# Attention and gated feed-forward on one Trainium2 core: one transpose per key tile for both halves, the second key tile filled by a DMA, the queries' halves swapped between the score tiles

## The chip, the cores and the metric

The kernel runs on one core of one Trainium2 chip. The metric is the device time of one execution in microseconds (us). Before the change the median of 3 runs is 1196.5 us (1196.28 to 1198.25).

## The reference

```python
def _L0_xattn_ref(hidden_q, kv_c, Wq, w_kc_q, w_kc_kv, W_qr, W_kr, Wo):
    q_big = jnp.einsum('bshk,hkq->bshq', (hidden_q @ Wq.T).reshape(b, s, H, K), w_kc_q)
    kv_rope = kv_c * cos[None] + _rotate_half(kv_c) * sin[None]
    q_r = jnp.einsum('bshq,hqr->bhsr', q_big, W_qr)
    k_r = jnp.einsum('bld,hdr->bhlr', kv_rope, W_kr)
    attn = jax.nn.softmax(jnp.einsum('bhsr,bhlr->bhsl', q_r, k_r), axis=-1)
    ctx_c = jnp.einsum('bhsl,bld->bhsd', attn, kv_rope)
    ctx_lat = jnp.einsum('bhsd,hkd->bshk', ctx_c, w_kc_kv)
    return ctx_lat.reshape(b, s, H * K) @ Wo.T
...
x = x + _L0_xattn_ref(_layernorm(x), ctx_512, ...)
x = x + _L0_ffn_ref(_layernorm(x), ...)
```

There are 8 batches of 256 queries of width 256. Each attends over 1601 keys of width 64, which all 16 heads share. The feed-forward part takes the last row of each batch through four gelu steps, spreads the result over the rows, gates it and normalises.

## The kernel before

At the start all weights are folded, so that a head's query is 64 wide and scores are a product with the rotated keys themselves. Scores are wanted more exactly than one 16-bit product gives, so keys and queries are split into a high f16 half and a low one (what the high half leaves), and a score is high·high + high·low + low·high.

The main loop runs over 8 batches (n), in each over 8 pairs of heads (p), in each over 13 tiles of 128 keys (t). A pair's queries fill 512 columns. For each tile TensorE issues, in this order, the scores (`L739` with `k_hi`, `L740` with `k_lo`, into `ps_s`), a product whose maximum over keys a later pair needs (`L610`, `L613`, into `ps_m`, read by VectorE at `L934`), perhaps one extra piece of work, and 12 products of probabilities with keys for the tile six steps back (`p_kv`, `L658`, `L661`, `L668`). ScalarE makes the probabilities (`L459`); their low halves are made by GpSimd on 11 tiles of 13 and by VectorE on the others (`make_low`, `L207`). PSUM bank `ps_x` is shared by the extra pieces; TensorE waits in `take_x` until its last user has read it.

GpSimd prepares the keys of the next batch between its other work (`keys`, `L311`, slots written out by hand in `KEY_SLOTS`): it rotates them and stores for each tile `k3` = [high 64, ones, low 64, the factor 16, 31 zeros], 162 columns. TensorE turns them in four pieces (`keys_turned`), placed by hand: piece 0 (high, tiles 0 to 7) at p 3, t 12; piece 1 (high, tiles 8 to 12) at p 5, t 6; pieces 2 and 3 (low) at p 6, t 6 and t 12. In pieces 0 and 1 each tile takes two transposes, `L544` to all 128 PSUM rows and `L545`, which writes the high half once more over rows 64 to 127. Pieces 2 and 3 take one transpose for each tile (`L547`). ScalarE copies each piece to SBUF (`copy_keys`). So `k_hi` holds [high; high] on 128 rows and `k_lo` holds [low; 16; zeros] on 96. The queries come to `qq` by DMAs that SyncE issues (`move_queries`): `qq[:, 0]` is [high; low] and `qq[:, 1]` is [high; negated maximum, by `copy_row`; zeros]. For batch 0 all this is done in the head of the kernel, in banks of their own.

The lines of `keys_turned` (TensorE), which the change touches most:

```python
if i < 2:
    pe.transpose(psum[:, c:c + 128], k3[par][:, t, 0:128], identh[:, :])
    mm = pe.transpose(psum[DC:128, c:c + 128], k3[par][:, t, 0:DC], identh[:, :])
else:
    mm = pe.transpose(psum[0:96, c:c + 128], k3[par][:, t, LOW:LOW + 96], identh[:, :])
```

Of the kernel before, what the change touches and what calls it, by code (L numbers as in the profile page):

```python
# [39 lines left out]
KC = 162  # L40
ONE, LOW, FACTOR = DC, DC + 1, 2 * DC + 1
# [13 lines left out]
def build_xattn_ffn(nc, x, kv, kv_last, cos_n, sin_n, ident_in, sel_in, wq, wkcq_t, wkckv, wqr, wkr_t, wo_t,  # L55
                    in_gamma, in_beta, agg_w, agg_b, pn_gamma, pn_beta, d1_w, d1_b, d2_w, d2_b,
                    bc_w, bc_b, gate_w, gate_b, out_gamma, out_beta, out):
    with ExitStack() as ctx:
# [19 lines left out]
        k_hi = [sb(f"k_hi{i}", [128, LP], F16) for i in range(2)]  # L78
        k_lo = [sb(f"k_lo{i}", [96, LP], F16) for i in range(2)]
# [80 lines left out]
        prep, kt_done, kt_copied = sem("prep"), sem("kt_done"), sem("kt_copied")  # L160
# [27 lines left out]
        def first_key_bank(i):  # L188

            return (ps_o[:, 0, :].bitcast(F16), ps_m[:, 0, :].bitcast(F16), ps_m[:, 1, :].bitcast(F16), ps_xh)[i]  # L190
# [34 lines left out]
        def _(sp):  # L225
# [18 lines left out]
            def move_queries(p, g):  # L244
# [5 lines left out]
                for h in range(2):  # L250
                    for j in range(2):
                        sp.dma_start(d[0:64, j, h * S:(h + 1) * S], q_hi[r][64 * h:64 * h + 64, :]).then_inc(in_qq[r], 16)
                sp.wait_ge(ql_done, g + 1)
                for h in range(2):
                    sp.dma_start(d[64:128, 0, h * S:(h + 1) * S], q_lo[r][64 * h:64 * h + 64, :]).then_inc(in_qq[r], 16)

            move_queries(0, 0)
            move_queries(1, 1)
            sp.dma_start(gw[:, :, :], gate_w.rearrange("(t p) m -> p t m", p=128)).then_inc(in_gate, 16)
# [10 lines left out]
            def batch(n, par):  # L270
# [7 lines left out]
                for p in range(NP - 2 if last(n) else NP):  # L278
                    move_queries((p + 2) % NP, n * NP + p + 2)

# [11 lines left out]
        def _(pool):  # L292
            def keys(n, par, k):
# [6 lines left out]
                else:  # L300
# [69 lines left out]
        def _(act):  # L370
# [70 lines left out]
            for i in range(4):  # L441
                copy_keys(0, 0, i, first_key_bank(i))
# [6 lines left out]
            def batch(n, par):  # L449
                for p in range(NP):  # L450
                    g = n * NP + p
                    started = not (first(n) and p == 0)
                    for t in range(KT):
# [6 lines left out]
                        if t == 6 and not last(n) and p in (5, 6):  # L460
                            copy_keys(n + 1, 1 - par, p - 4)
# [7 lines left out]
                        if t == 12 and not last(n) and p in (3, 6):  # L469
                            copy_keys(n + 1, 1 - par, 0 if p == 3 else 3)  # L470
# [65 lines left out]
        def _(pe):  # L536
            def keys_turned(n, par, i, psum=ps_xh):

                pe.wait_ge(prep, n * PREP_OPS + (6 if i % 2 == 0 else 12))
                for t in range(8) if i % 2 == 0 else range(8, KT):  # L540
                    c = (t % 8) * 128
                    if i < 2:

                        pe.transpose(psum[:, c:c + 128], k3[par][:, t, 0:128], identh[:, :])  # L544
                        mm = pe.transpose(psum[DC:128, c:c + 128], k3[par][:, t, 0:DC], identh[:, :])  # L545
                    else:
                        mm = pe.transpose(psum[0:96, c:c + 128], k3[par][:, t, LOW:LOW + 96], identh[:, :])  # L547
                mm.then_inc(kt_done, 1)

# [35 lines left out]
            for i in range(3):  # L585
                keys_turned(0, 0, i, first_key_bank(i))
# [15 lines left out]
            def maxima(par, p, g, j):  # L602
# [4 lines left out]
                if j < MX_OPS - 1:  # L607
                    a = (j // 3) * 128
                    c = (j % 3) * 512
                    mm = pe.matmul(ps_m[:, j % 3, :], qq[p % 4][:, 0, a:a + 128], k_hi[par][:, c:c + 512], start=True, stop=True)  # L610
                else:
                    for i in range(4):
                        mm = pe.matmul(ps_m[:, 1, i * LAST:(i + 1) * LAST], qq[p % 4][:, 0, i * 128:(i + 1) * 128],  # L613
                                       k_hi[par][:, L - LAST:L], start=True, stop=True)
# [15 lines left out]
            keys_turned(0, 0, 3)  # L630
            pe.wait_ge(kt_copied, 3)
# [11 lines left out]
            pe.wait_ge(kt_copied, 4)  # L643
# [6 lines left out]
            def p_kv(n, par, p, t):  # L650
# [9 lines left out]
                for q in range(4):  # L660
                    pe.matmul(d[:, q // 2, q % 2, 0:DC], probs_hi(t)[:, q * 128:(q + 1) * 128], k3[par][:, t, LOW:LOW + DC],  # L661
# [53 lines left out]
            def batch(n, par):  # L715
# [9 lines left out]
                for p in range(NP):  # L725
# [3 lines left out]
                    for t in range(KT):  # L729
# [3 lines left out]
                        if t == 0:  # L733
                            pe.wait_ge(mrow_copied, g + 1)
                            if p == 0 and not first(n):
                                pe.wait_ge(kt_copied, n * 4 + 4)
# [7 lines left out]
                        if t >= KT - EARLY and not (last(n) and p >= NP - 2):  # L744
                            if t == KT - EARLY:
                                pe.wait_ge(in_qq[p % 2], n * (QQ_DMAS * 4) + QQ_DMAS * ((p + 2) // 2 + 1))
                                if p == NP - 2:
                                    pe.wait_ge(kt_copied, n * 4 + 6)
# [4 lines left out]
                        if t == 6 and not last(n) and p in (5, 6):  # L753
                            take_x((kt_copied, n * 4 + (4 + p - 3)))
                            keys_turned(n + 1, 1 - par, p - 4)
# [9 lines left out]
                        if t == 12:  # L765
# [88 lines left out]
        def _(dve):  # L854
# [371 lines left out]
```

## Time and profile before

| what | value |
| --- | --- |
| runs | 1196.28, 1196.5, 1198.25 us, median 1196.5 |
| the profiled execution | 1192.87 us |
| its span, first to last instruction | 1191.1 us |
| mean granted TensorE clock | 0.961 of full |
| TensorE busy | 1104.9 us, 93% |
| GpSimd, VectorE, ScalarE busy | 889.8, 882.1 and 670.9 us |

The engines are named PE (TensorE matmul), PEld (its weight load), DVE (VectorE), ACT (ScalarE), POOL (GpSimd), SP (SyncE). L547 is line 547 of the kernel. The ends of matmuls are modelled, so that back-to-back ones overlap in the records: the cost of one is the distance between starts, not its duration. Idle time of an engine that sets nothing costs nothing.

### The profile page before, as it was taken

Reading aid. Unit: us, or ns where it says so; the run is one execution under the profiler, and the core shown is the slowest. Engines: PE = TensorE matmul, PEld = TensorE weight load, DVE = VectorE, ACT = ScalarE, POOL = GpSimd, SP = SyncE. Lnnn points to the kernel's source line nnn. Section 1 sums busy time; section 2 is a strip of 40 time slices with the busy share of each in tenths; the row PEclk is TensorE's granted clock in tenths of the full one; section 3 lists DMA queues with packets and bytes.
Section 4 is the critical chain, followed back from the end, with each engine's and each line's share of the span. In section 5 each row is a group of like instructions: output and inputs, shape, how many; then the busy total and the mean of one; then the engine's idle time right before and its main releaser. Section 6 shows DMA issues by size and latency. Waiting matters only on the chain.

```text
span 1191.1 us, 39790 instructions
## 1 busy us (share of the span) xinstructions
PE 1104.9 (93%) x14852; PEld 735.9 (62%) x14852; DVE 882.1 (74%) x1573; ACT 670.9 (56%) x1195; POOL 889.8 (75%) x956
## 2 busy tenths in 40 slices
PE   5879999999999998999999999999999999999361
PEld 4636666666666665666666666666676666667240
DVE  4377778777787777777878687777877787887448
ACT  1445566566665665565656665566656565567322
POOL 0329887898788976798788877897879877787713
PEclk9989999999999999999999999999999999999655
DMA  9020001000100001000100001000100020000002
GB/s 331 40 78 14 14 14 27 14 16 15 30 16 14 12 14 33 14 14 12 30 16 16 15 16 29 12 15 16 29 13 13 14 86 16 15 15 3 1 2 71
DMA packets 41288, 34.69 MB, mean 29 GB/s; under 512 B 7608, under 2 KB 38648, under 8 KB 40640
## 3 DMA queue, kind: packets, MB, share of 16 engines
q1 hardware_dynamic: 40512, 27.79, 8.3%
q10 hardware_dynamic: 576, 4.19, 1.0%
q8 instruction: 130, 2.13, 0.7%
q14 instruction: 70, 0.57, 0.2%
HBM read 17.27 MB, written 2.10 MB: 16 GB/s over the span
## 4 chain that ended last, share of the span: by engine, by line
PE 85%; DVE 7%; issue 3%; DMA 2%; ACT 1%; POOL 1%; SPq 1%; DVEq 0%; ACTq 0%; POOLq 0%
PE ps_s L740 14%; PE ps_s L739 14%; PE ps_m L610 13%; PE ps_o L658 8%; PE ps_o L661 8%; PE ps_o L668 8%; PE ps_x L598 3%; PE ps_x L684 3%; PE ps_x L621 2%; DVE mx L934 1%; PE ps_x L545 1%; PE ps_x L676 1%; PE ps_x L544 1%; DMA plo_all<-wqr_dram 1%; PE ps_x L711 1%
## 5 line engine op out<-in xcount | busy, mean ns | idle before, releaser
L207 POOL TENSOR_TENSOR plo_all<-big 128x512 f16<-128x512 f32 x640 | 683.3, 1085 | 213.8 <-ACT big L459 213.0
L934 DVE TENSOR_REDUCE mx<-ps_m 128x1 f32<-128x512 f32 (+1 forms) x832 | 544.7, 666 | 218.6 <-PE ps_m L610 188.2
L459 ACT ACTIVATE big<-ps_s 128x512 f32<-128x512 f32 x768 | 458.4, 598 | 342.2 <-PE ps_s L740 341.1
L739 PE MATMUL ps_s<-qq,k_hi 128*128 128x512 f16 (+1 forms) x832 | 316.2, 380 | 5.6 <-issue 5.6
L740 PE MATMUL ps_s<-qq,k_lo 96*128 96x512 f16 (+1 forms) x832 | 318.0, 382 | 0.0
L610 PE MATMUL ps_m<-k_hi,qq 128*128 128x512 f16 x768 | 293.1, 382 | 5.1 <-ACT k_lo L378 2.3
L658 PEld LDWEIGHTS ps_o<-k,big 128*128 128x128 bf16 x3072 | 184.9, 98 | 119.8 <-issue 1.1
L661 PE MATMUL ps_o<-k,big 128*128 128x64 f16 x3072 | 219.8, 193 | 0.0
L668 PE MATMUL ps_o<-k,plo_all 128*128 128x65 f16 x3072 | 218.2, 193 | 0.0
L658 PE MATMUL ps_o<-k,big 128*128 128x65 f16 x3072 | 218.1, 193 | 0.0
L207 DVE TENSOR_TENSOR plo_all<-big 128x512 f16<-128x512 f32 x128 | 172.3, 1346 | 0.0
L661 PEld LDWEIGHTS ps_o<-k,big 128*128 128x128 bf16 x3072 | 146.5, 98 | 0.0
L668 PEld LDWEIGHTS ps_o<-k,plo_all 128*128 128x128 f16 x3072 | 144.8, 97 | 0.1
L610 PEld LDWEIGHTS ps_m<-k_hi,qq 128*128 128x128 f16 x768 | 76.0, 99 | 103.6 <-DVE mx L934 9.9
L739 PEld LDWEIGHTS ps_s<-qq,k_hi 128*128 128x128 f16 (+1 forms) x832 | 81.7, 98 | 7.4 <-issue 6.9
L740 PEld LDWEIGHTS ps_s<-qq,k_lo 96*128 96x128 f16 (+1 forms) x832 | 82.4, 99 | 0.9 <-issue 0.6
L311 POOL TENSOR_TENSOR tables<-tables 128x256 f32<-128x256 f32 (+3 forms) x64 | 60.6, 947 | 27.7 <-DMA tables<-kv_last_dram 27.1
L207 POOL TENSOR_TENSOR plo_last<-pr_last 65x512 f16<-65x512 f32 x64 | 66.3, 1036 | 0.9 <-ACT pr_last L459 0.9
L598 PE MATMUL ps_x<-xnt,mw 128*128 (+1 forms) x384 | 52.2, 272 | 2.4 <-DVE mw L913 1.4
L598 PEld LDWEIGHTS ps_x<-xnt,mw 128*128 128x128 f16 x384 | 37.1, 97 | 20.9 <-DVE mw L913 1.6
L459 ACT ACTIVATE pr_last<-ps_s 65x512 f32<-65x512 f32 x64 | 38.0, 594 | 13.9 <-PE ps_s L740 13.6
L378 ACT ACTIVATE qq<-ps_x 1x512 f16<-1x512 f32 x64 | 37.7, 589 | 5.8 <-PE ps_x L621 4.2
(200 smaller groups left out, 998.4 us busy)
## 6 DMA issues: line engine op xcount, KB each, us to landing
qq<-q_hi SPq DMA_DIRECT2D x256, 32.0 KB, 1.9
qq<-q_lo SPq DMA_DIRECT2D x128, 32.0 KB, 1.9
tables<-kv_dram SPq DMA_DIRECT2D x8, 384.0 KB
big<-wq_dram ACTq DMA_DIRECT2D x1, 2048.0 KB, 15.5
xs<-x_dram SPq DMA_DIRECT2D x4, 512.0 KB, 18.0
big<-wo_t_dram SPq DMA_DIRECT2D x1, 2048.0 KB, 13.1
tables<-d_w_dram SPq DMA_DIRECT2D x2, 1024.0 KB, 6.9
out_dram<-big SPq DMA_DIRECT2D x8, 256.0 KB, 2.2
```

What stands on the lines that cost most here:

```text
L207: eng.tensor_tensor(probs_lo(t)[0:r, :], probs(t)[0:r, :], probs_hi(t)[0:r, :], ALU.subtract).then_inc(done, 1)
L311: pool.tensor_tensor(*ops[k % 6]).then_inc(prep, 1)
L378: return act.activation(out_, in_, ACT.Copy, **kw)
L459: act.activation(probs(t)[0:r, :], ps_s[0:r, (p * KT + t) % 2, :], ACT.Exp, scale=1.0 / SC).then_inc(p_done, 1)
L598: mm = pe.matmul(ps_x[:, 0:S], mw[wi][:, mt, p * 128:(p + 1) * 128], xn_hl[xi][:, bass.ds(n * S + mt * B * S, S)], start=(i == 0), stop=(i ...
L610: mm = pe.matmul(ps_m[:, j % 3, :], qq[p % 4][:, 0, a:a + 128], k_hi[par][:, c:c + 512], start=True, stop=True)
L658: pe.matmul(d[:, q // 2, q % 2, :], probs_hi(t)[:, q * 128:(q + 1) * 128], k3[par][:, t, 0:OW], start=(t == 0 and q == 0), stop=False, ski ...
L661: pe.matmul(d[:, q // 2, q % 2, 0:DC], probs_hi(t)[:, q * 128:(q + 1) * 128], k3[par][:, t, LOW:LOW + DC], start=False, stop=False, skip_g ...
L668: mm = pe.matmul(d[:, q // 2, q % 2, :], probs_lo(t)[:, q * 128:(q + 1) * 128], k3[par][:, t, 0:OW], start=False, stop=(t == KT - 1), skip ...
L739: pe.matmul(ps_s[0:r, j % 2, :], k_hi[par][:, c], qq[p % 4][:, 0, :], start=True, stop=False)
L740: pe.matmul(ps_s[0:r, j % 2, :], k_lo[par][:, c], qq[p % 4][0:96, 1, :], start=False, stop=True).then_inc(st_done, 1)
L934: dve.tensor_reduce(o, i, AX.X, ALU.max).then_inc(mx_read, 1)
```

## The change

The tile `k3` becomes [ones, high 64, low 64], 130 columns, so that high and low lie side by side. One transpose for each key tile gives [high; low] on 128 rows; pieces 2 and 3 and the second transposes are gone, and with them half of ScalarE's key copies. `k_hl` takes the place of `k_hi`. `k_hx`, in the place of `k_lo`, is [high; 16; zeros]: its high rows are filled by a DMA from `k_hl`, issued by SyncE after each copy (`move_keys`), its other 32 rows are written once at the start. The queries are swapped to fit: `qq[:, 0]` is [high; high], `qq[:, 1]` is [low; negated maximum; zeros]. The first scores of a batch wait for the DMAs (`in_kx`) instead of the copies. The maxima are now taken over high·high + low·high instead of high·high + high·low.

```diff
-KC = 162
-ONE, LOW, FACTOR = DC, DC + 1, 2 * DC + 1
+KC = 130
+ONE, HIGH, LOW = 0, 1, DC + 1
...
-        k_hi = [sb(f"k_hi{i}", [128, LP], F16) for i in range(2)]
-        k_lo = [sb(f"k_lo{i}", [96, LP], F16) for i in range(2)]
+        k_hl = [sb(f"k_hl{i}", [128, LP], F16) for i in range(2)]
+        k_hx = [sb(f"k_hx{i}", [96, LP], F16) for i in range(2)]
...
                     for j in range(2):
-                        sp.dma_start(d[0:64, j, h * S:(h + 1) * S], q_hi[r][64 * h:64 * h + 64, :]).then_inc(in_qq[r], 16)
+                        sp.dma_start(d[64 * j:64 * j + 64, 0, h * S:(h + 1) * S], q_hi[r][64 * h:64 * h + 64, :]).then_inc(in_qq[r], 16)
                 sp.wait_ge(ql_done, g + 1)
                 for h in range(2):
-                    sp.dma_start(d[64:128, 0, h * S:(h + 1) * S], q_lo[r][64 * h:64 * h + 64, :]).then_inc(in_qq[r], 16)
+                    sp.dma_start(d[0:64, 1, h * S:(h + 1) * S], q_lo[r][64 * h:64 * h + 64, :]).then_inc(in_qq[r], 16)
+
+            def move_keys(n, par, i):
+                sp.wait_ge(kt_copied, n * 2 + (i + 1))
+                sp.dma_start(k_hx[par][0:64, key_half(i)], k_hl[par][0:64, key_half(i)]).then_inc(in_kx, 16)
...
             move_queries(1, 1)
+            for i in range(2):
+                move_keys(0, 0, i)
...
+                    if not last(n) and p in (3, 5):
+                        move_keys(n + 1, 1 - par, (p - 3) // 2)
...
-                    (k3[par][:, c, 0:DC], raw[:, c, :], rot[:, c, :], ALU.add),
+                    (k3[par][:, c, HIGH:HIGH + DC], raw[:, c, :], rot[:, c, :], ALU.add),
                     (raw[:, c, :], raw[:, c, :], rot[:, c, :], ALU.add),
-                    (k3[par][:, c, LOW:LOW + DC], raw[:, c, :], k3[par][:, c, 0:DC], ALU.subtract),
+                    (k3[par][:, c, LOW:LOW + DC], raw[:, c, :], k3[par][:, c, HIGH:HIGH + DC], ALU.subtract),
...
-                act.wait_ge(kt_done, n * 4 + (i + 1))
-                c = slice(0, 1024) if i % 2 == 0 else slice(1024, LP)
-                d = k_hi[par] if i < 2 else k_lo[par]
-                r = 128 if i < 2 else 96
-                copy(d[0:r, c], psum[0:r, 0:c.stop - c.start]).then_inc(kt_copied, 1)
+                act.wait_ge(kt_done, n * 2 + (i + 1))
+                c = key_half(i)
+                copy(k_hl[par][:, c], psum[:, 0:c.stop - c.start]).then_inc(kt_copied, 1)
...
-                        if t == 6 and not last(n) and p in (5, 6):
-                            copy_keys(n + 1, 1 - par, p - 4)
+                        if t == 6 and not last(n) and p == 5:
+                            copy_keys(n + 1, 1 - par, 1)
...
-                        if t == 12 and not last(n) and p in (3, 6):
-                            copy_keys(n + 1, 1 - par, 0 if p == 3 else 3)
+                        if t == 12 and not last(n) and p == 3:
+                            copy_keys(n + 1, 1 - par, 0)
...
-                pe.wait_ge(prep, n * PREP_OPS + (6 if i % 2 == 0 else 12))
-                for t in range(8) if i % 2 == 0 else range(8, KT):
+                pe.wait_ge(prep, n * PREP_OPS + 6 * (i + 1))
+                for t in range(KT)[HALVES[i]]:
                     c = (t % 8) * 128
-                    if i < 2:
-
-                        pe.transpose(psum[:, c:c + 128], k3[par][:, t, 0:128], identh[:, :])
-                        mm = pe.transpose(psum[DC:128, c:c + 128], k3[par][:, t, 0:DC], identh[:, :])
-                    else:
-                        mm = pe.transpose(psum[0:96, c:c + 128], k3[par][:, t, LOW:LOW + 96], identh[:, :])
+                    mm = pe.transpose(psum[:, c:c + 128], k3[par][:, t, HIGH:HIGH + 128], identh[:, :])
...
-            for i in range(3):
+            for i in range(2):
...
-            keys_turned(0, 0, 3)
-            pe.wait_ge(kt_copied, 3)
+            pe.wait_ge(kt_copied, 2)
             pe.wait_ge(in_qq[0], QQ_DMAS)
...
+                            if p == 0:
+                                pe.wait_ge(in_kx, n * 32 + 32)
...
-                        pe.matmul(ps_s[0:r, j % 2, :], k_hi[par][:, c], qq[p % 4][:, 0, :], start=True, stop=False)
-                        pe.matmul(ps_s[0:r, j % 2, :], k_lo[par][:, c], qq[p % 4][0:96, 1, :], start=False, stop=True).then_inc(st_done, 1)
+                        pe.matmul(ps_s[0:r, j % 2, :], k_hl[par][:, c], qq[p % 4][:, 0, :], start=True, stop=False)
+                        pe.matmul(ps_s[0:r, j % 2, :], k_hx[par][:, c], qq[p % 4][0:96, 1, :], start=False, stop=True).then_inc(st_done, 1)
...
-                            elif p in (3, 6) and not last(n):
-                                i = 0 if p == 3 else 3
-                                take_x((kt_copied, n * 4 + (4 + i + 1)))
-                                keys_turned(n + 1, 1 - par, i)
+                            elif p == 3 and not last(n):
+                                take_x((kt_copied, n * 2 + 3))
+                                keys_turned(n + 1, 1 - par, 0)
...
-                pad(k3[i][:, :, FACTOR:FACTOR + 1], SC)
-                pad(k3[i][:, :, FACTOR + 1:KC], 0.0)
+                pad(k_hx[i][64:96, :], 0.0)
+            for i in range(2):
+                pad(k_hx[i][64:65, :], SC, 7)
```

## Rows read from the trace of the kernel before

**Rows 1.** The page's busy times: engine, us (share of the span), instructions.

```profile
PE 1104.9 (93%) x14852; PEld 735.9 (62%) x14852; DVE 882.1 (74%) x1573; ACT 670.9 (56%) x1195; POOL 889.8 (75%) x956
```

**Rows 2.** A window: busy us of PE, PEld, DVE, ACT, POOL, granted clock, DMA share, GB/s.

```profile
208.00:336.00 128.00, 127.68 (x1778) 85.50 (x1777) 98.99 (x171) 77.77 (x139) 106.33 (x114) 1.00 0.07 18
```

**Rows 3.** Waits of TensorE from 100 to 1095 us: total, times, longest.

```profile
PE ps_s L739 <- issue: 5.6, 2, 3.0
PE ps_x L676 <- DVE ctx_m L957: 1.6, 7, 0.2
```

**Rows 4.** Timeline of TensorE around pieces 0 and 1 (keys for batch 1): start, us, what.

```profile
137.18 0.22 PE L544 MATMUL ps_x<-identh,k 128*128 128x128 f16 x1
137.33 0.24 PE L545 MATMUL ps_x<-identh,k 128*64 128x128 f16 x1
...
139.86 0.29 PE L658 MATMUL ps_o<-k,big 128*128 128x65 f16 x4
...
162.30 0.23 PE L544 MATMUL ps_x<-identh,k 128*128 128x128 f16 x1
...
163.98 0.20 PE L658 MATMUL ps_o<-k,big 128*128 128x65 f16 x1
```

**Rows 5.** The chain that ended last, at pieces 2 and 3: start, us on it.

```profile
178.56 0.45 PE ps_x L547 x8
...
185.65 0.28 PE ps_x L547 x5
```

**Rows 6.** Weight loads of L547 and of L544: ns min/median/max.

```profile
L547 PEld LDWEIGHTS ps_x<-identh,k x96: 120/124/125, 62.0 to 964.0; 128*96 128x96 f16 x96
...
L544 PEld LDWEIGHTS ps_x<-identh,k x91: 95/96/97, 137.0 to 940.2; 128*128 128x128 f16 x91
```

**Rows 7.** Timeline of the head, TensorE and GpSimd.

```profile
36.69 0.92 POOL L311 TENSOR_TENSOR k<-tables 128x320 f16<-128x320 f32 x1
...
38.64 0.78 POOL L311 TENSOR_TENSOR k<-tables,k 128x320 f16<-128x320 f32 x1
...
46.76 0.22 PE L544 MATMUL ps_o<-identh,k 128*128 128x128 f16 x1 [0.74 <-issue]
...
51.81 3.42 PE L590 MATMUL ps_s<-plo_all,nw 128*128 128x128 f32 x16
...
58.43 0.83 PE L598 MATMUL ps_x<-xnt,mw 128*128 128x256 f16 x6 [1.42 <-DVE mw L913]
```

**Rows 8.** A window of the head, columns as in rows 2.

```profile
51.80:55.00 3.20, 3.20 (x18) 3.20 (x17) 0.50 (x1) 0.60 (x1) 0.00 (x0) 0.54 0.00 0
```

**Rows 9.** VectorE in the head: its wait for the input, its memsets (ns min/median/max).

```profile
DVE st_f L878 <- DMA xs<-x_dram: 13.7, 1, 13.7
...
L858 DVE MEMSET qq<- x4: 272/272/272, 2.7 to 3.6; 32x256 uint32 x4
```

**Rows 10.** Timeline of batch 1, pairs 3 to 5: GpSimd's lead over TensorE.

```profile
271.02 1.04 POOL L207 TENSOR_TENSOR plo_all<-big 128x512 f16<-128x512 f32 x1 [0.77 <-ACT big L459]
...
273.33 2.04 POOL L207 TENSOR_TENSOR plo_all<-big 128x512 f16<-128x512 f32 x2
...
278.49 0.28 PE L668 MATMUL ps_o<-k,plo_all 128*128 128x65 f16 x4
```

**Rows 11.** Timeline of batch 1: copies, query DMAs, the tile that needs them.

```profile
266.40 1.02 ACT L378 ACTIVATE k_hi<-ps_x 128x1024 f16<-128x1024 f16 x1 [2.20 <-PE ps_x L545]
...
271.22 0.39 ACT L378 ACTIVATE q_hi<-ps_x 128x256 f16<-128x256 f32 x1 [0.28 <-PE ps_x L598]
...
286.55 2.39 SPq L252 DMA_DIRECT2D qq<-q_hi  x4
288.99 1.23 SPq L255 DMA_DIRECT2D qq<-q_lo  x2
...
294.55 0.38 PE L610 MATMUL ps_m<-k_hi,qq 128*128 128x512 f16 x1
```

**Rows 12.** Landing of the query DMAs, all of the span.

```profile
DMA to landing us min/median/max: 1.7/1.9/3.5
```

More of the change, by code:

```diff
@@ L159, in build_xattn_ffn @@
             sem(s) for s in ("ln", "ln_dev", "xn_act", "xn_dve", "xt_done", "xt_copied", "xt_low"))
-        prep, kt_done, kt_copied = sem("prep"), sem("kt_done"), sem("kt_copied")
+        prep, kt_done, kt_copied, in_kx = (sem(s) for s in ("prep", "kt_done", "kt_copied", "in_kx"))
         q_done, qh_done, ql_done = sem("q_done"), sem("qh_done"), sem("ql_done")
@@ L188, in first_key_bank, with key_half @@
         def first_key_bank(i):
-            return (ps_o[:, 0, :].bitcast(F16), ps_m[:, 0, :].bitcast(F16), ps_m[:, 1, :].bitcast(F16), ps_xh)[i]
+            return (ps_o[:, 0, :].bitcast(F16), ps_m[:, 0, :].bitcast(F16))[i]
+        def key_half(i):
+            return slice(0, 1024) if i == 0 else slice(1024, LP)
         def sums(r):
@@ L440, in _ @@
             high_part(1, 1)
-            for i in range(4):
+            for i in range(2):
                 copy_keys(0, 0, i, first_key_bank(i))
@@ L609, in maxima @@
                     c = (j % 3) * 512
-                    mm = pe.matmul(ps_m[:, j % 3, :], qq[p % 4][:, 0, a:a + 128], k_hi[par][:, c:c + 512], start=True, stop=True)
+                    mm = pe.matmul(ps_m[:, j % 3, :], qq[p % 4][:, 0, a:a + 128], k_hl[par][:, c:c + 512], start=True, stop=True)
                 else:
@@ L613, in maxima @@
                         mm = pe.matmul(ps_m[:, 1, i * LAST:(i + 1) * LAST], qq[p % 4][:, 0, i * 128:(i + 1) * 128],
-                                       k_hi[par][:, L - LAST:L], start=True, stop=True)
+                                       k_hl[par][:, L - LAST:L], start=True, stop=True)
                 mm.then_inc(mx_done, 1)
@@ L642, in _ @@
                         mm.then_inc(fold, 1)
-            pe.wait_ge(kt_copied, 4)
             max_row(0)
@@ L660, in p_kv @@
                 for q in range(4):
-                    pe.matmul(d[:, q // 2, q % 2, 0:DC], probs_hi(t)[:, q * 128:(q + 1) * 128], k3[par][:, t, LOW:LOW + DC],
+                    pe.matmul(d[:, q // 2, q % 2, HIGH:OW], probs_hi(t)[:, q * 128:(q + 1) * 128], k3[par][:, t, LOW:LOW + DC],
                               start=False, stop=False, skip_group_check=True)
@@ L747, in batch @@
                                 if p == NP - 2:
-                                    pe.wait_ge(kt_copied, n * 4 + 6)
+                                    pe.wait_ge(kt_copied, n * 2 + 4)
                             maxima(par if p < NP - 2 else 1 - par, p + 2, g + 2, t - (KT - EARLY))
@@ L752, in batch @@
                             project(1 - par, (1,))
-                        if t == 6 and not last(n) and p in (5, 6):
-                            take_x((kt_copied, n * 4 + (4 + p - 3)))
-                            keys_turned(n + 1, 1 - par, p - 4)
+                        if t == 6 and not last(n) and p == 5:
+                            take_x((kt_copied, n * 2 + 4))
+                            keys_turned(n + 1, 1 - par, 1)
                         if t == 3 and not (last(n) and p >= NP - 2):
@@ L864, in _ @@
                 pad(k3[i][:, :, ONE:ONE + 1], 1.0)
-                pad(k3[i][:, :, FACTOR:FACTOR + 1], SC)
-                pad(k3[i][:, :, FACTOR + 1:KC], 0.0)
+                pad(k_hx[i][64:96, :], 0.0)
+            for i in range(2):
+                pad(k_hx[i][64:65, :], SC, 7)
             for i in range(4):
@@ L956, in normalise @@
                 dve.wait_ge(inv_done, g + 1)
-                dve.tensor_tensor(ctx_m[:, :, :, :].rearrange("p s h d -> p h s d"), d[:, :, :, 0:DC],
+                dve.tensor_tensor(ctx_m[:, :, :, :].rearrange("p s h d -> p h s d"), d[:, :, :, HIGH:OW],
                                   inv[:, :, :].unsqueeze(3).to_broadcast([128, 2, ST, DC]), ALU.mult).then_inc(ctx_norm, 1)
```

2 lines of the change are left out of this document (removed).

## The prediction

> **What bounds the kernel now.** I read the page's busy times first [rows 1]: TensorE is busy for 93% of the span, the next engine for 75%. A share over the span can hide a stage with another limit, so I cut out a stretch of one batch's length [rows 2]: TensorE is busy for 127.68 of 128 us at full clock, GpSimd for 106.33, VectorE for 98.99, ScalarE for 77.77. The waits of TensorE between 100 and 1095 us, nearly the whole main loop, settle it [rows 3]: 5.6 us where it waits for nothing that the trace shows (two gaps), and 1.6 us for VectorE in seven waits of 0.2 us. So in the loop TensorE's own work sets the time: what is taken off it comes off the end, as long as the others keep up. The reader is to see that nobody else's removed work counts there.
>
> The last thing to read is how much the removed work takes. Matmul records overlap, so I take distances between starts. Piece 0 (8 tiles, 16 transposes) begins at 137.18 and the next kind of work at 139.86: 2.68 us. Piece 1 (5 tiles, 10 transposes) goes from 162.30 to 163.98: 1.68 us [rows 4]. Both are 0.335 us for each pair of transposes, or 0.168 us each. Pieces 2 and 3, with one transpose for each tile, stand in the chain that ended last with 0.45 us for 8 and 0.28 us for 5 [rows 5], 0.056 us each. The alternation between L544 over all rows and L545 over the upper 64 makes a transpose three times as dear as in an unbroken run of like ones.
>
> **The change, part by part.**
>
> *Transposes in the loop.* Pieces 0 and 1 stay, with one transpose for each tile, in an unbroken run into the same rows: the form of pieces 2 and 3, so 0.45 and 0.28 us. The old pieces 2 and 3 go. A batch saves (2.68 - 0.45) + (1.68 - 0.28) + 0.45 + 0.28 = 4.36 us. Keys are turned in the loop for 7 batches: 7 x 4.36 = 30.5 us.
>
> What isn't seen in the trace is the new transpose itself: 128 columns wide as its weights go and starting one element into the row. The nearest row is L547: 96 wide, starting at element 65, also odd. Its weight load takes 124 ns and that of L544, 128 wide at an even start, 96 ns [rows 6]; at a spacing of 56 ns the former is evidently hidden behind the stream before. I take 56 ns. From one side, the most that a cheaper one could give is all of it, 13 x 0.056 x 8 = 5.8 us. From the other, the old mean of 168 ns would cost 13 x 0.112 x 8 = 11.6 us. The middle case, loads of 124 ns one after another, is a rival below.
>
> On that spacing the Trainium skill speaks against me: its page "TensorE: Matmul & The Clock Gate", section "Back-to-back issue gap", gives about 81 ns for a matmul of 128 columns in a stream of weight load and matmul pairs, against about 56 ns for an isolated gap. This trace has 56 ns for just such pairs of transposes. By the page's 81 ns the 104 new transposes would cost an estimated 104 x 0.025 = 2.6 us more.
>
> *Transposes in the head.* The four pieces of batch 0 lie between 46.76, the first, and 51.81, where the fold that follows begins [rows 7] (of piece 3, five transposes, issued later, I say nothing: it lies before a wait for DMAs). That is 5.05 us for 34 transposes; the 13 new ones take 0.73. The keys themselves were ready at 39.4, so GpSimd isn't what is waited for, and the chain goes on from the fold by way of ScalarE and VectorE to the queries at 58.43, which all move forward with it. I take 4.3 us. The clock was granted at 0.54 in the window of the fold [rows 8], so the same work could take some 1.5 us less or, where a fall comes at another place, more. I keep 4.3 and put 1.5 us on both sides.
>
> *ScalarE.* Two of four key copies go, 14 in the loop of about 1.0 or 0.7 us. ScalarE is busy for 78 of 128 us [rows 2] and TensorE doesn't wait for it [rows 3]: nothing. In the head the two first copies end earlier, but the queries' DMAs stand in the same wait: nothing.
>
> *GpSimd's key operations.* Same count and sizes. The high half is now written at an odd element. The low half always was, and its operation takes 0.78 us where the even one takes 0.92 [rows 7], so I see no price. If there were one, GpSimd would pay it out of the slack reckoned below.
>
> *Memsets.* Two of 32 x 1664 and two of 1 x 1664 f16 come, against four small ones. 32 x 256 words take 0.27 us [rows 9], so 832 words take about 0.85 us each, 3.4 us in all; VectorE then waits 13.7 us for the input [rows 9], and GpSimd starts the keys only after their own load. Nothing. Without that cover it would be 3 us, once.
>
> *The DMAs.* Two more for each batch, 128 and 80 KB, are issued on SyncE's queue behind the queries of pairs 3 and 5. SyncE waits there for the copy of the keys. Behind it stand the queries of the next pair. In batch 1 the copy ends at 267.42, and the next queries are ready to move at 271.61 [rows 11]: SyncE is free again 4.2 us before, less 0.6 us for issuing one DMA (four take 2.39). The wait of TensorE for them comes at the first tile of the next batch, two pairs or more later, against 1.9 us, at most 3.5, for a landing of 32 KB [rows 12]. Even four times the longest is well inside. In the head they are issued after the queries of pair 1 and are needed after the 13 maxima of pair 0: hidden too.
>
> *What comes nearer to binding.* GpSimd, at pairs 3 to 5, where four key operations and the root's steps stand. Piece 0 gets shorter by 2.23 us, so TensorE comes that much sooner. GpSimd has 0.77 us of idle time before 271.02 which it can use up [rows 10], so its lead falls by about 1.5 us. The low half of tile 4 is ready at 274.35 (the first of the two from 273.33) and used at 278.49: a lead of 4.1 us, which falls to about 2.7. It holds, and over the batch GpSimd has 106 us of work in the 123.6 that remain. VectorE has 99. The query DMAs: the last of pair 5 is issued at 290.22, lands at about 292.1, and is used at 294.55 [rows 11, 12]; piece 1 takes 1.4 us out of that, leaving about 1.0, which is what pairs without a piece have today. TensorE's wait for in_qq costs nothing in those [rows 3].
>
> **The sum.** 30.5 + 4.3 = 34.8 us. The profiled execution took 1192.87 us, 1.8 around its span; it would be 1158.1. The median of the runs is 3.6 us above it: 1196.5 - 34.8 = 1161.7 us.
>
> **The rivals.** *The weight loads don't hide.* The new transposes are 128 wide at an odd start; if each waits for a load like L547's 124 ns, 104 x 0.068 = 7.1 us are lost: 1168.8 us. For it: the load is the longer of the two. Against it: the same load hides today. By the 81 ns that the Trainium skill's page "TensorE: Matmul & The Clock Gate" gives in that section, a weaker form of this, it would be an estimated 1164.3 us.
>
> *The cover gives way.* GpSimd's low halves come late after piece 0. From the point where its lead is under 2.2 us instead of 4.1, TensorE waits once a batch for what is missing, at most the 2.23 us saved there: 15.6 us in all, 1177.3 us; half of it is 1169.5. For it: 83% busy against the 75% that the page shows. Against it: the lead above.
>
> *All given back.* Another engine's round for a pair is the true beat and TensorE's work only fills it. It would be 1196 us. Rows 3 speak against it: TensorE would have idled somewhere.
>
> *Slower, by SyncE's queue.* A move of keys holds up the queries behind it. It is free if it ends in the 4.2 us; each us over that, and over the 1.0 us that the queries have in hand, is a us of waiting at the maxima. With 14 moves it eats the gain only if each is late by 2.5 us beyond both, about 7.7 us after the copy, and ends slower beyond: at 9 us after the copy, 14 x (9 - 5.2) = 53 us, 1215 us. A landing of 3.5 us at most [rows 12] speaks against it.
>
> **How the numbers follow.** Forecast 0.76, unhidden loads 0.08, cover gives way in part 0.10, all given back 0.03, slower 0.03. The range goes from 1157.5 (1.5 us for the head's clock, and a part of the 5.8) to 1169.5, where the unhidden loads and half of the lost cover lie. A difference of 0.2%, 2.4 us, is about what can be told from none. Faster 0.94, same 0.03, slower 0.03.
>
> **What would show it.** TensorE with 104 transposes of keys, all of one form and 56 ns apart; pieces of 0.45 and 0.28 us, and a batch of about 123.3 us; still no wait of TensorE in the loop above 2 us in sum; the fold in the head beginning at about 47.5. Wrong if the transposes stand 80 ns or more apart, if L668 waits for GpSimd or L610 for a query DMA once a batch, or if the first scores of a batch wait for k_hx.

## The result, and the profile after

The kernel after takes 1167.5 us in the median of 4 runs (1164.5 to 1168.2), against 1196.4 us of the kernel before. The ratio is 0.9751, with a 95% interval from 0.9731 to 0.9771. 28.9 us are saved where 34.8 were forecast. The profiled execution took 1167.40 us, 25.5 less than that of before.

The page of the kernel after, its busy times, answers to [rows 1]:

```profile
PE 1073.1 (92%) x14644; PEld 714.8 (61%) x14644; DVE 886.5 (76%) x1573; ACT 657.9 (56%) x1179; POOL 890.4 (76%) x956
```

TensorE has 208 instructions less and 32 us less of work. GpSimd has what it had; VectorE has 4 us more, about what the four memsets of `k_hx` at the start take (0.75 to 1.45 us each). The timeline of TensorE in the kernel after, at piece 0 and at piece 1, answers to [rows 4, 5]:

```profile
128.67 0.61 PE L552 MATMUL ps_x<-identh,k 128*128 128x128 f16 x8
129.11 0.28 PE L660 MATMUL ps_o<-k,big 128*128 128x65 f16 x4
...
273.73 0.38 PE L614 MATMUL ps_m<-k_hl,qq 128*128 128x512 f16 x1
274.29 0.45 PE L552 MATMUL ps_x<-identh,k 128*128 128x128 f16 x5 [0.19 <-DVE q_lo L925]
274.58 0.28 PE L660 MATMUL ps_o<-k,big 128*128 128x65 f16 x4
```

Eight transposes take 0.44 us and five 0.29, 55 to 58 ns each, at an odd start and 128 columns wide. Ahead of piece 1 stands something new: its first transpose could have begun at 273.95, one spacing of 0.22 us after L614, and begins at 274.29, 0.34 us late. It waits for VectorE's low queries. Now the waits of TensorE in the loop, from 90 to 1070 us, as in [rows 3]:

```profile
PE ps_s L741 <- issue: 12.6, 2, 6.7
PE ps_x L678 <- DVE ctx_m L959: 1.6, 7, 0.2
PE ps_m L614 <- DMA qq<-q_lo: 1.6, 4, 0.6
PE ps_x L552 <- DVE q_lo L925: 0.9, 5, 0.2
```

The first line had 5.6 us in [rows 3]. It is two gaps again, and they have more than doubled. The third line is new: small waits for query DMAs, the two of 0.6 us in the pairs that follow the gaps. The chain that ended last, in the kernel after, goes straight through one of them:

```profile
436.10 0.60 ACT pr_last L469
436.70 5.87 issue
442.57 0.61 PE ps_s L741
443.18 0.43 PE ps_s L742
```

And windows of the gap and of what follows (columns as in rows 2):

```profile
436.50:442.50 6.00, 0.14 (x5) 0.02 (x1) 0.60 (x2) 0.19 (x1) 1.31 (x2) 0.80 0.06 15
442.50:447.00 4.50, 4.43 (x32) 2.49 (x33) 1.38 (x2) 1.20 (x2) 1.71 (x2) 0.51 0.01 4
447.00:452.00 5.00, 5.00 (x69) 3.30 (x67) 4.16 (x6) 2.77 (x5) 2.68 (x4) 1.00 0.05 13
```

TensorE stands still, with nothing that the profile shows holding it, and the others nearly so (GpSimd, the busiest, works for 1.31 of 6 us). Behind the gap TensorE runs at half clock (0.51 granted, the 1.2 GHz level) for about 4.5 us. The place is where TensorE's instruction stream returns to the top of its loop: the 8 batches are batch 0, a loop of three rounds of two batches, and batch 7, so the loop returns before batches 3 and 5. The traffic of the kernel after in that gap (436.4 to 442.6) is instruction fetch, on two queues:

```profile
q14 instruction: 7, 0.06, 3.5%
q8 instruction: 2, 0.03, 2.5%
```

Which of them is TensorE's can be told from the pages of the straight kernels below. With TensorE alone in a straight line q8 has 116 packets in the whole execution for the 129 of the kernel after, and q14 has 70 as before. With all engines in a straight line q14 has 42, and q8 stays at 116. So q8 fetches TensorE's instructions, and q14 those of other engines: in the kernel after with TensorE straight, the same window again holds 7 packets of q14, and TensorE works on.

To see where the whole difference went, I took the starts of the query products, one for each pair at its tile 3, and compared the distances (us, pair by pair, in the profiled executions):

```
interval that holds                    before          after
piece 0 (pair 3), 7 batches            17.09 to 17.34  14.85 to 14.86
piece 1 (pair 5), batches 1 to 5       17.81           16.75 to 16.77
the same, batch 0; batch 6             16.35; 17.81    14.95; 16.43
old pieces 2 and 3 at pair 6           15.13 to 15.14  14.40 to 14.41
first pair of batch 0                  14.70          13.10
loop return before batch 3             19.21           22.56, next pair 15.17 for 14.40
loop return before batch 5             17.13           23.70, next pair 15.16 for 14.40
pairs with none of these               equal within 0.4, most within 0.02
```

| term | forecast | in the profiled executions |
| --- | --- | --- |
| pieces in the loop | 30.5 | 15.9 + 8.1 + 5.1 = 29.1 |
| head, first key transpose (46.76; 45.27) to first scores (79.39; 72.30) | 4.3 | 5.6 |
| pair 0 of batch 0 (14.70; 13.10) | 0 | 1.6 |
| start of the first key transpose (arrival of inputs) | 0 | 1.5 |
| the two loop returns with the pair behind each | 0 | -11.5 |
| the rest | 0 | -0.8 |
| sum | 34.8 | 25.5 |

The start of the first key transpose is chance: it lies between 45.27 and 46.89 us in the profiles of the kernel after and its variants.

Against the medians the step at the loop is smaller, since other runs of the kernel before took about 1196 us and its profiled one only 1192.87.

### The profile page after: what moved, and what is told of

The parts are those of the page before. It is cut to its first block, busy times and chain, and to the rows that moved or that the text cites. A ratio compares the mean times of both kernels' runs of the same rounds, so it can differ in the third digit from the quotient of the medians.

```text
span 1165.6 us, 39347 instructions
## 1 busy us (share of the span) xinstructions
PE 1073.1 (92%) x14644; PEld 714.8 (61%) x14644; DVE 886.5 (76%) x1573; ACT 657.9 (56%) x1179; POOL 890.4 (76%) x956
## 4 chain that ended last, share of the span: by engine, by line
PE 81%; DVE 8%; issue 4%; DMA 4%; SPq 2%; ACT 1%; POOL 1%; DVEq 0%; ACTq 0%; POOLq 0%
PE ps_s L742 14%; PE ps_s L741 14%; PE ps_m L614 13%; PE ps_o L660 8%; PE ps_o L663 8%; PE ps_o L670 8%; PE ps_x L602 3%; PE ps_x L686 3%; DMA qq<-q_lo 2%; DVE mx L936 2%; PE ps_x L625 2%; SPq L255 1%; PE ps_x L678 1%; PE ps_x L713 1%; DMA plo_all<-wqr_dram 1%
## 5 line engine op out<-in xcount | busy, mean ns | idle before, releaser
L741 PE MATMUL ps_s<-qq,k_hl 128*128 128x512 f16 (+1 forms) x832 | 317.3, 381 | 12.6 <-issue 12.6
L742 PE MATMUL ps_s<-qq,k_hx 96*128 96x512 f16 (+1 forms) x832 | 319.0, 383 | 0.0
L614 PE MATMUL ps_m<-k_hl,qq 128*128 128x512 f16 x768 | 293.8, 383 | 6.7 <-DMA qq<-q_lo 5.5
L614 PEld LDWEIGHTS ps_m<-k_hl,qq 128*128 128x128 f16 x768 | 76.4, 100 | 107.6 <-DVE mx L936 13.9
L741 PEld LDWEIGHTS ps_s<-qq,k_hl 128*128 128x128 f16 (+1 forms) x832 | 81.7, 98 | 14.4 <-issue 13.8
L742 PEld LDWEIGHTS ps_s<-qq,k_hx 96*128 96x128 f16 (+1 forms) x832 | 82.6, 99 | 1.0 <-issue 0.8
L323 POOL TENSOR_TENSOR tables<-tables 128x256 f32<-128x256 f32 (+3 forms) x64 | 55.1, 861 | 27.1 <-DMA tables<-kv_last_dram 26.5
```

What stands on the lines that cost most here:

```text
L323: pool.tensor_tensor(*ops[k % 6]).then_inc(prep, 1)
L741: pe.matmul(ps_s[0:r, j % 2, :], k_hl[par][:, c], qq[p % 4][:, 0, :], start=True, stop=False)
L742: pe.matmul(ps_s[0:r, j % 2, :], k_hx[par][:, c], qq[p % 4][0:96, 1, :], start=False, stop=True).then_inc(st_done, 1)
```

## The experiments

The theories. **A**: the transposes are worth what was forecast, and what is missing went into TensorE's return to the top of its loop. **B**: it is the new wait for `k_hx` at that place, or a loss spread over the loop. In the diffs "..." stands for lines or text left out.

**TensorE in a straight line**, in the kernel after:

```diff
-            batches(pe, batch)
+            for n in range(B):
+                batch(n, n % 2)
```

> The kernel after, with TensorE's 8 batches written out in a straight line; the other four engines keep their loop. Theory A: the missing microseconds are TensorE's return to the top of its loop, before batches 3 and 5, where it stood still for 5.9 and 6.7 us and then ran at half the clock (the two pairs took 8.2 and 9.3 us more than the others, and each next pair 0.8 us more). Then both gaps go, no pair 0 takes over 14.6 us, and the time falls by 17 to 19 us to about 1150. Theory B: the gap is the wait for k_hx at the first tile of a batch, or the loss is spread over the loop: the gaps stay, and the time is within 3 us of 1167.5.

Measured: 1151.5 us (1150.0 to 1152.6), ratio to the kernel before 0.9632 (0.9608 to 0.9656). The gaps are gone; the intervals of 22.56 and 23.70 us are 15.42 and 15.41. A holds. It had said 14.6 at most, though, and 17 to 19 us for the 16.0 measured: 1.0 us stays at each place, most of it a wait of TensorE for ScalarE (0.85 and 0.83 us), which here still has its loop. TensorE's waits from 90 to 1055 us have no "issue" any more; the longest is

```profile
PE ps_s L741 <- ACT big L469: 1.7, 2, 0.8
```

**The same in the kernel before**:

> The kernel before, with TensorE's 8 batches in a straight line. Theory A: its two gaps (3.0 and 2.6 us in the profiled run, pairs 4.8 and 2.7 us too long) go as well, and the time falls by 7 to 12 us to 1185 to 1189. The difference to the straight form of the kernel after is then the transposes alone: 30.5 in the loop less 1.8 for a wait on the low queries, and 4 to 7 in the head, 33 to 36 us. Theory B: no fall in either, and a difference of 29 us as between the looped kernels.

Measured: 1188.7 us (1185.6 to 1189.6), ratio 0.9945 (0.9922 to 0.9968). So the loop costs the kernel before 7.3 us and the kernel after 16.0, and without it the change is worth 1188.7 - 1151.5 = 37.2 us by the medians, a little above the 33 to 36 expected, and 33.9 us by the two profiled executions. In these it is 958.1 against 928.7 us from the query product of pair 1 in batch 0 to the last one, 29.5 for the 30.5 of the forecast.

**The order of the transposes**, in the kernel before: all first ones of a piece, then all second ones.

```diff
+                    for t in ts:
...
                         pe.transpose(psum[:, c:c + 128], k3[par][:, t, 0:128], identh[:, :])
+                    for t in ts:
...
                         mm = pe.transpose(psum[DC:128, c:c + 128], k3[par][:, t, 0:DC], identh[:, :])
```

> The kernel before, with the same transposes of pieces 0 and 1 in another order: first all onto 128 rows, then all second ones onto rows 64 to 127. Theory A: the alternation is what makes them dear, and in two runs each takes 0.056 us: piece 0 takes 0.9 us and piece 1 0.56 instead of 2.68 and 1.68, which is 2.9 us a batch, 20.4 in the loop and 2.9 in the head: 1173 us. Theory B: the transposes onto the upper rows are dear in themselves, about 0.28 us each: the pieces stay at 2.7 and 1.7 us and the time at 1196.

Measured: 1213.4 us (1212.6 to 1215.8), ratio 1.0157 (1.0130 to 1.0183): slower, against both theories. The transposes did get cheap: the timeline of TensorE has this for the second half of piece 0,

```profile
257.16 0.63 PE L547 MATMUL ps_x<-identh,k 128*64 128x128 f16 x8
257.73 0.29 PE L662 MATMUL ps_o<-k,big 128*128 128x65 f16 x4
```

8 in 0.57 us, 71 ns each, and the interval with piece 0 fell from 17.09 to 15.53 us. It is the alternation that was dear. But pair 4, which follows, took 21.0 to 21.9 us instead of 14.84 in batches 1 to 6, because of a wait for VectorE. That is 40.1 us in all, and 1213.4 less 40.1 is 1173.3, where theory A had expected the kernel. The timelines of VectorE and of GpSimd in that run:

```profile
262.61 7.84 DVE L207 TENSOR_TENSOR plo_all<-big 128x512 f16<-128x512 f32 x1
```

```profile
261.23 3.03 POOL L207 TENSOR_TENSOR plo_all<-big 128x512 f16<-128x512 f32 x3
264.23 0.86 POOL L311 TENSOR_TENSOR tables<-tables 128x320 f32<-128x320 f32 x1
265.06 2.03 POOL L207 TENSOR_TENSOR plo_all<-big 128x512 f16<-128x512 f32 x2
267.05 0.85 POOL L311 TENSOR_TENSOR k<-tables 128x320 f16<-128x320 f32 x1
267.87 2.03 POOL L207 TENSOR_TENSOR plo_all<-big 128x512 f16<-128x512 f32 x2
273.94 1.04 POOL L207 TENSOR_TENSOR plo_all<-big 128x512 f16<-128x512 f32 x1 [4.04 <-ACT big L459]
```

A low half of VectorE that takes 0.68 to 2.2 us elsewhere in this run, mostly 1.4, lasts 7.84 us, from within an unbroken stretch of GpSimd's work to its end at 269.90 and a little beyond. Both engines read two operands in SBUF. I called this **theory C**: the operation gets no turn while GpSimd has no pause, and it depends on where in the stretch it begins. The missing pause alone isn't enough: in the kernel after GpSimd works unbroken from 253.03 to 279.12, and the low halves that VectorE begins at 256.21, 264.10 and 271.05 last 0.93, 1.14 and 2.18 us. The first of these is the one that answers to the stalled one, 0.71 us behind the start of GpSimd's three low halves where the stalled one began 1.38 us behind it. But the second begins 1.45 us behind the start of such a group and isn't stalled, so the distance alone doesn't decide it either. The Trainium skill, page "SBUF — State Buffer", section "SBUF: two separate sides", has a lock on the ports that the two engines share, held for a whole instruction by whoever starts first. The trace agrees that one blocks the other, but VectorE stood here through more than six instructions of GpSimd.

**The second transposes put back**, in the kernel after:

```diff
-                    mm = pe.transpose(psum[:, c:c + 128], k3[par][:, t, HIGH:HIGH + 128], identh[:, :])
+                    pe.transpose(psum[:, c:c + 128], k3[par][:, t, HIGH:HIGH + 128], identh[:, :])
+                    mm = pe.transpose(psum[DC:128, c:c + 128], k3[par][:, t, HIGH:HIGH + DC], identh[:, :])
```

> The kernel after, with a second transpose of each key tile put back behind the first, onto rows 64 to 127, as before (these rows then hold the high half, so the products with the low half of the keys are lost). Theory A: 13 pairs a batch at 0.335 us instead of 13 transposes at 0.056 us: 3.6 us a batch, 25.4 in the loop and 3.6 in the head, 1196 us; everything but the transposes (copies, DMAs, swapped queries) is worth nothing. Theory B: they cost what a like one costs, 5.8 us in all, 1173 us.

Measured: 1187.1 us (1186.6 to 1191.9). Theory A had said 1196, theory B 1173. The intervals of pieces 0 and 1 are those of the kernel before, 17.10 and 17.82 us, so the pairs of transposes cost 2.25 and 1.07 us a batch over the kernel after, and with the 0.34 us of waiting whose place they take nearly the 3.6 expected. It isn't 1196 because the loop returns are short again (18.93 and 19.52 us for 22.56 and 23.70, and 0.8 less behind each): 9.3 us, and 1196.5 - 9.3 = 1187.2. That this agrees to 0.1 us is in part luck: the loop gave 23.8 us for the 25.4 expected and the head 5.1 for the 3.6.

**Theory C tried by position**: 12 more transposes in each piece 0, to shift what follows by the 0.67 us that the slow run was late.

```diff
-                    mm = pe.transpose(...)
+                    for _ in range((3 if t < 4 else 2) if i == 0 and not first(n) else 1):
+                        mm = pe.transpose(...)
```

> The kernel after, with 12 more transposes of the same form and place in piece 0 of the keys for batches 1 to 7 (20 instead of 8), so that piece 0 takes 1.12 us, as long as in the run with the two runs of transposes, instead of 0.45. Theory C: what made that run slow is the position of VectorE's low half of tile 2 of pair 4 within an unbroken stretch of GpSimd's work: it lasted 7.8 us there, 0.93 us in the kernel after, and TensorE waited at the maxima for 4 to 5 us. The same shift by 0.67 us then brings it back here: pair 4 takes 21 to 22 us instead of 14.85, and the time is 1167.5 + 4.7 + 6 x 6.5, about 1211 us. Theory D: it had to do with the second transposes or the kernel before only: the time rises by 7 x 0.67 = 4.7 us to 1172.

Measured: 1202.4 us, widely spread (1195.9 to 1208.9, 10 runs), below the 1211 of theory C and far above the 1172 of theory D. In the profiled execution, at 1205.8 us, pair 4 takes 21.1 to 22.5 us in all six batches. The timeline of VectorE, and after it the tile that TensorE is late with:

```profile
258.47 7.84 DVE L210 TENSOR_TENSOR plo_all<-big 128x512 f16<-128x512 f32 x1
```

```profile
266.97 0.61 PE L615 MATMUL ps_m<-k_hl,qq 128*128 128x512 f16 x1 [4.64 <-DVE mx L937]
```

D falls: a shift of 0.67 us in a kernel that has none of the second transposes brings the stall back.

**And by GpSimd's stretch**: the same kernel, with GpSimd's last key operations later.

```diff
-             (3, 4): 6, (3, 12): 7, (4, 3): 8, (4, 5): 9, (4, 8): 10, (4, 12): 11}
+             (3, 4): 6, (3, 12): 7, (4, 8): 8, (4, 10): 9, (4, 12): 10, (5, 1): 11}
```

> The kernel with 12 more transposes in piece 0, which took 1202 us with a low half of VectorE lasting up to 7.8 us in pair 4, and GpSimd's last four key operations moved from tiles 3, 5, 8 and 12 of pair 4 to tiles 8, 10 and 12 of pair 4 and tile 1 of pair 5. Theory C: the operation is long because GpSimd works without a pause from before it until it ends, 261 to 270 us; with the key operations gone from there a pause comes after two or three low halves, VectorE's operation is back under 3 us, pair 4 under 16 us, and the time falls by 6 x 6.5 to about 1164 to 1172. Rival: the length comes from the position against TensorE's or ScalarE's work alone: it stays at 7.8 us and the time at 1200.

Measured: 1187.5 us (1180.3 to 1195.7, 10 runs), not the 1164 to 1172 that theory C gave. Pair 4 is back at 14.84 to 14.87 us, and its low half lasts 2.18 us and ends with the first pause of GpSimd: there C holds, and the rival with 7.8 us falls. But the backlog now stands at the turn to pair 5, and the same thing happens to the next low half in batches 2 to 6, where piece 1 waits for the low queries behind it (21.6 to 23.0 us for 16.4). VectorE and TensorE in that run:

```profile
396.91 5.53 DVE L210 TENSOR_TENSOR plo_all<-big 128x512 f16<-128x512 f32 x1
```

```profile
403.51 0.71 PE L553 MATMUL ps_x<-identh,k 128*128 128x128 f16 x5 [3.54 <-DVE q_lo L926]
```

The stall goes where GpSimd's unbroken stretch goes; it wasn't removed. In all seventeen stalls of the three profiles (six, six and five) the operation ends 0.55 us after GpSimd's stretch does; which start inside a stretch gets a turn before that stays open.

**Theory B, the wait for k_hx**, moved to the last tile of the batch before:

```diff
-                            if p == 0:
-                                pe.wait_ge(in_kx, n * 32 + 32)
+                            if p == 0 and first(n):
+                                pe.wait_ge(in_kx, 32)
...
+                        if t == 12 and p == NP - 1 and not last(n):
+                            pe.wait_ge(in_kx, n * 32 + 64)
```

> The kernel after, looped, with the wait for k_hx moved from the first tile of a batch to the last tile of the batch before. Theory A: TensorE's gap at the return of its loop is no wait on a semaphore: it stays, 1165 to 1168 us. Rival: the wait for k_hx with a computed count, the only new instruction at that place, made the gap grow from 3 to 6 us: it falls back to 3 us, and the time by 8 to 10 us to 1158.

Measured: 1166.5 us (1165.3 to 1168.8), gaps of 5.33 and 6.46 us. B falls.

**The kernel after once more.**

> The kernel after once more, for a second look at the gap at the return of TensorE's loop (5.9 and 6.7 us in the first). If it depends on the program it is again 5 to 7 us; if on the moment, it is somewhere between 2 and 7 us. The time within 1164 to 1169 us.

Measured: 1167.0 us (one run), gaps of 5.90 and 6.51 us. The gap belongs to the program, not to the moment.

**What in the program.** 12 more transposes, once in batch 0 only (ahead of the loop), once in the loop's two batches only:

```diff
+                    for _ in range((4 if t < 10 else 3) if i == 1 and isinstance(n, int) and n == 1 else 1):
```

```diff
+                    for _ in range((4 if t < 10 else 3) if i == 1 and not isinstance(n, int) else 1):
```

> The kernel after, looped, with 12 more like transposes in piece 1 of batch 0 alone (executed once, 0.7 us): the loop of TensorE is as long as in the kernel after but lies 24 instructions later in the program. Theory F: the gap at the loop's return (5.9 and 6.7 us; 3.6 and 3.6 with 12 more transposes in every piece 0) depends on where the loop lies: it changes, to about 3.6 us, and with it goes the half clock behind it: 1167.5 + 0.7 - 7 = 1161. Theory G: it depends on the loop's own length, or on what else is in flight: it stays at 6 us and more, 1168 us.

> The kernel after, with 12 more like transposes in piece 1 of each of the two batches in TensorE's loop (executed six times, 4.0 us) and none before the loop: the loop begins where it does in the kernel after and is 48 instructions longer. Theory F: the position is the same, so the gap stays at about 6 us: 1171.5 us. Theory G: the length counts: the gap is 3.6 us, 1164.5 us. Pair 4 stays at 14.85 us in either, since piece 0 is unchanged.

Measured: 1157.65 us (1157.5 to 1158.9), ratio to the kernel before 0.9686 (0.9667 to 0.9705), for the first; 1171.1 us (1169.0 to 1171.8) for the second. F holds: twelve useless transposes ahead of the loop make the kernel 9.9 us faster. In the first run the gaps are 3.12 and 3.33 us, about the 3.6 that it gave, but the time is 3.4 us under its 1161; in the second the gaps are 6.30 and 6.12 us and the time is within 0.4 us of its 1171.5. F had said too that the half clock behind the gap would go; it has only become shorter (0.62 granted in the 4 us behind the first gap). TensorE at the first return, in the timelines of the first and of the second:

```profile
441.02 0.61 PE L742 MATMUL ps_s<-qq,k_hl 128*128 128x512 f16 x1 [3.12 <-issue]
```

```profile
444.81 0.61 PE L742 MATMUL ps_s<-qq,k_hl 128*128 128x512 f16 x1 [6.30 <-issue]
```

The ten profiles of looped kernels fall in two groups: gaps of 2.55 to 3.71 us (the kernel before and five variants) or of 5.33 to 6.67 us (the kernel after, its repetition, the moved wait, the longer loop). TensorE's fetch queue tells them apart. In each of the eight long gaps it has two packets of 16 KB, the second begun 3.1 to 3.6 us after the first, and TensorE goes on 1.3 to 1.6 us after the second has ended. In each of the twelve short ones it has one, and TensorE goes on 1.7 to 2.2 us after its end. The window 437.6 to 441.05 of the run with the transposes ahead of the loop has

```profile
q8 instruction: 1, 0.02, 2.1%
```

against the 2 packets shown for the kernel after.

**Versions to keep.** Piece 1 moved from pair 5 to pair 6 in the straight kernel:

```diff
-                    if not last(n) and p in (3, 5):
-                        move_keys(n + 1, 1 - par, (p - 3) // 2)
+                    if not last(n) and p in (3, 6):
+                        move_keys(n + 1, 1 - par, (p - 3) // 3)
...
-                        if t == 6 and not last(n) and p == 5:
+                        if t == 6 and not last(n) and p == 6:
```

> The kernel after with TensorE in a straight line, and piece 1 of the keys (transposes, copy, DMA) moved from tile 6 of pair 5 to tile 6 of pair 6. Theory E: at pair 5 piece 1 waits 0.2 to 0.35 us for VectorE's low queries, because VectorE has just spent 2.2 us on a low half beside GpSimd's backlog of pair 4; at pair 6 GpSimd has idle time and piece 1 waits for nothing. It saves 0.25 us a batch, 1.7 us: 1149.8 against 1151.5. Rival: the wait goes with the piece, or another takes its place at pair 6: 1151.5.

Measured: 1149.2 us (1148.7 to 1150.7); the wait for the low queries is gone, the interval with piece 1 is 14.69 us, 0.28 above an empty one. 2.3 us against the straight kernel, at the edge of what the spreads of the two tell.

**All five engines in a straight line**:

> The fastest so far (TensorE in a straight line, piece 1 at pair 6, 1149.2 us), with the other four engines in a straight line as well. If their return to the top of the loop costs TensorE anything (pair 0 of batches 3 and 5 still takes 15.5 us instead of 14.4), both go to 14.4 and the time to 1147. If not, 1149.

Measured: 1147.2 us (1145.3 to 1148.3), ratio to the kernel before 0.9597 (0.9580 to 0.9614). The two intervals at the loop returns, 15.52 and 15.46 us before, are 14.41: the other engines' returns cost TensorE 1.1 us each, too. It is the fastest version, 20 us ahead of the kernel after. TensorE's waits in its loop, from 90 to 1050 us, are down to

```profile
PE ps_x L675 <- DVE ctx_m L957: 1.6, 7, 0.2
PE ps_m L611 <- DMA qq<-q_lo: 0.2, 1, 0.2
```

## Why the prediction was right, and where it was off

The direction and the range were right and the mechanism was the forecast one: TensorE was the bound, and its transposes came off the end. The size was off by 5.9 us of 34.8, and the sum was right only in part for its reasons: in the profiled executions 3.1 us that nobody had forecast (pair 0 of batch 0, and the chance start of the transposes) stand against 11.5 us lost at the loop.

*Transposes in the loop.* 30.5 forecast, 29.1 in the profiled executions, 29.5 between the straight kernels. A batch takes 124.4 us for the 123.3 forecast (128 less 4.36 would have been 123.6). The new transpose costs 55 to 58 ns, so the rival of unhidden loads falls. The Trainium skill, page "TensorE: Matmul & The Clock Gate", section "Back-to-back issue gap", has about 81 ns for a matmul of 128 columns in a stream of weight loads and matmuls; this trace doesn't agree, and the measurement decides. The load of the new form took 98 ns, not the 124 of L547. The other rows of the change, two copies, the swapped queries, the DMAs, are worth nothing that shows: with the second transposes put back, the kernel after has the intervals of the kernel before at pieces 0 and 1.

*The lead of the others.* I had reckoned GpSimd's lead over TensorE and found it enough; it was: TensorE never waited for GpSimd in the loop. But I had asked only whether GpSimd itself would be late, not whom it holds up. The 0.34 us before piece 1 in batches 1 to 5 (1.7 us in all) are VectorE, late after a low half of 2.18 us at 271.05 beside GpSimd's backlog (1.72 us at the same place before). The rival "the cover gives way" had the wrong engine and too low a price: 2.2 us a batch at most, where over 6 us proved possible. With the small waits for query DMAs, TensorE waited 4.1 us in the loop apart from the gaps, where the prediction had given 2 us at most as a sign. From the kernel with 12 more transposes in piece 0: the kernel after is 0.67 us of phase away from losing 6.3 to 7.6 us in each of six batches.

*The head.* 4.3 forecast, 5.6 measured; the 4.3 are there (5.05 us from the first transpose to the fold before, 0.72 after), and the rest is the fold, whose first 16 matmuls took 3.42 us before, at half clock, and 2.00 in the kernel after. That is the 1.5 that was put on both sides. The two DMAs of keys were issued from 60.13 on and landed within 3.6 us, 7 us and more before the first scores at 72.30. In pair 0 of batch 0 the kernel before waited 1.4 us once for a query DMA and the kernel after not (that pair takes 14.4 to 14.7 us in the three profiles with the old keys and 13.1 in all others); why was not tried.

*The step that failed* is the reading of [rows 3]: "5.6 us where it waits for nothing that the trace shows (two gaps)" was left in the sum as a constant. It was the cost of the loop's return, and it is set by where the loop lies in TensorE's program, so that taking out instructions, any instructions, could change it. The term is worth -8.7 us by the medians of straight and looped kernels (7.3 before, 16.0 after). That 37.2 - 8.7 is 28.5, near the 28.9 measured, proves nothing, since all these differences are taken from the same four medians; the proof is that the gaps go with the loop. That position and neither the wait, nor the loop's length, nor the moment sets the term is shown. That TensorE waits there for its instructions, for one packet in a short gap and for two, one after the other, in a long one, is argued from the fetch queue, which agrees in all twenty gaps; no run changed the fetch by itself. Which position is a good one stays open.

*SyncE's queue.* Right: no query waited behind a move of keys. The issues of k_hx took 0.46 to 0.60 us and landed in 2.0 to 3.6 us, 2.2 in the median.

## What to carry to other kernels

An idle time that the profile puts down to nothing, at a place where an engine's loop returns, is not a constant: read its length and the clock behind it, and give it a price of its own in both signs whenever a change adds or removes instructions ahead of the loop. Where an engine is the bound and its gaps are few, write its stream out straight, or at least try the loop at another position. And where two engines both read SBUF operands, ask of each long unbroken stretch of one which operation of the other begins inside it.

## What was not expected of the hardware

- The return to the top of TensorE's loop cost 2.6 to 3.7 us in six programs and 5.3 to 6.7 us in three others (one of them profiled twice); behind the gap of 5.9 us the granted clock was at its lower level (0.51 in a window of 4.5 us). In every long gap TensorE's instruction fetch had two packets of 16 KB, in every short one one. The Trainium skill, page "Advanced Engine Details and Errata", section "Control Flow Timing", has about 51 ns for an unconditional branch and about 108 ns for a compare-and-branch; no return here was near either.
- Twelve transposes added ahead of a loop made the kernel 9.9 us faster (1167.5 to 1157.65).
- Alternating a transpose onto 128 rows with one onto the upper 64 costs 168 ns each; in two unbroken runs the same transposes cost 67 to 80 ns, and the new ones in one run 55 to 58.
- A low half of VectorE lasted 0.93 us or 7.84 us, depending on a shift of 0.67 us against GpSimd's unbroken work.
